# First layer norm scaled on ScalarE with a bias from GpSimd, and low parts of x subtracted on GpSimd

## The reference, cut to what matters

```python
x = _layernorm(x + _L0_attn_ref(x, w_in, w_out), axis=-1)
x = _layernorm(x + _L0_ffn_ref(x, wf, uf, bf, wi, ui, bi, wc, uc, bc, wo, uo, bo, in_c), axis=-1)

def _layernorm(x, axis=-1, eps=1e-05):
    m = jnp.mean(x, axis=axis, keepdims=True)
    v = jnp.var(x, axis=axis, keepdims=True)
    return (x - m) / jnp.sqrt(v + eps)
```

## Time and profile before

| what | value |
|---|---|
| median of 3 runs | 1065.08 us (1063.71 to 1067.06) |
| the profiled execution | 1063.56 us, span 1061.8 us, mean granted clock 0.966 |
| PE busy | 941.6 us, 89% of the span |
| DVE busy | 766.2 us, 72% |
| ACT busy | 551.6 us, 52% |
| POOL busy | 361.9 us, 34% |

### The profile page before, as it was taken

The page is one execution under the profiler, slowest core; times in us unless marked ns, Lnnn a source line. Parts: engine busy times, 40 slices in busy tenths (PEclk is TensorE's granted clock), DMA queues, the critical chain, the costliest instruction groups (busy, mean ns, idle before and its releaser), DMA issues.

```text
span 1061.8 us, 22111 instructions
## 1 busy us (share of the span) xinstructions
PE 941.6 (89%) x7576; PEld 710.8 (67%) x7576; DVE 766.2 (72%) x2882; ACT 551.6 (52%) x1101; POOL 361.9 (34%) x621
## 2 busy tenths in 40 slices
PE   3278899999999999999999999999999989788995
PEld 2155667676767676767676767676767757567884
DVE  6367667878786868686868686868787777336885
ACT  5044545555555555555555555555555454414876
POOL 2024333333333333333333333334343333300443
PEclk9688989999999999999999999999999999899998
DMA  6845353535353544445353536262626240103664
GB/s 191 188 136 153 114 152 92 159 94 157 104 150 111 140 121 119 142 111 151 99 158 93 157 88 160 84 176 81 180 61 165 77 100 2 41 20 99 189 209 139
DMA packets 92942, 131.74 MB, mean 124 GB/s; under 512 B 12008, under 2 KB 46696, under 8 KB 92832
## 3 DMA queue, kind: packets, MB, share of 16 engines
q1 hardware_dynamic: 92832, 130.34, 43.5%
HBM read 78.84 MB, written 50.33 MB: 122 GB/s over the span
## 4 chain that ended last, share of the span: by engine, by line
PE 57%; DVE 17%; ACT 9%; POOL 6%; issue 5%; SPq 3%; DMA 2%; ACTq 0%; POOLq 0%; DVEq 0%
PE bank L868 34%; PE bank L925 8%; PE bank L884 7%; DVE bank L652 5%; PE bank L906 3%; PE bank L933 3%; POOL Pt L348 2%; ACT Pt L427 2%; POOL Pt L350 2%; DVE y L694 2%; PE bank L964 2%; DVE gate L707 2%; DVE max_q L652 1%; ACT oT L444 1%; DVE c L709 1%
## 5 line engine op out<-in xcount | busy, mean ns | idle before, releaser
L652 DVE CUSTOM_DVE_ANT_0 bank<-bank,mask 128x256 f32<-128x256 f32 (+1 forms) x1024 | 368.7, 422 | 155.3 <-PE bank L884 154.1
L348 POOL TENSOR_SCALAR_AFFINE_SELECT Pt<-Pt 128x512 f32<-128x512 f32 x256 | 169.4, 662 | 588.0 <-ACT Pt L427 588.0
L427 ACT ACTIVATE Pt<-bank 128x512 f32<-128x512 f32 (+1 forms) x512 | 250.9, 545 | 170.0 <-PE bank L906 169.9
L884 PE MATMUL bank<-Ks,Qs 58*128 58x256 f32 (+1 forms) x1024 | 141.5, 336 | 43.6 <-DMA Ks<-parts_dram 23.4
L884 PEld LDWEIGHTS bank<-Ks,Qs 58*128 58x128 f32 x1024 | 84.1, 189 | 130.4 <-issue 88.0
L868 PE MATMUL bank<-x1T,Wg 128*128 128x512 f32 x576 | 158.6, 412 | 1.6 <-DVE x1T L625 1.6
L868 PE MATMUL bank<-cT,Ug 128*128 128x512 f32 x576 | 152.0, 401 | 3.7 <-DVE cT L625 3.7
L350 POOL TENSOR_SCALAR_AFFINE_SELECT Pt<-Pt 128x384 f32<-128x384 f32 x256 | 149.3, 583 | 0.0
L652 DVE DVE_READ_ACCUMULATOR2_ANT max_q<- 128x1 f32 x1024 | 144.3, 141 | 0.0
L925 PE MATMUL bank<-Pt,Vp 128*32 128x256 f32 (+1 forms) x2048 | 115.7, 369 | 12.1 <-POOL Pt L350 12.0
L868 PEld LDWEIGHTS bank<-cT,Ug 128*128 128x128 f32 x576 | 106.0, 190 | 26.2 <-DVE cT L625 4.1
(11 more groups left out here) (101 smaller groups left out, 1121.4 us busy)
## 6 DMA issues: line engine op xcount, KB each, us to landing
parts_dram<-qk_parts SPq DMA_DIRECT2D x128, 256.0 KB
Qs<-parts_dram SPq DMA_DIRECT2D x128, 128.0 KB, 2.6
Ks<-parts_dram SPq DMA_DIRECT2D x128, 128.0 KB, 2.8
xt_raw<-in_xt SPq DMA_DIRECT2D x16, 512.0 KB, 3.8
Qs<-parts_dram SPq DMA_DIRECT2D x128, 64.0 KB, 2.6
Ks<-parts_dram SPq DMA_DIRECT2D x128, 64.0 KB, 2.7
x_res<-in_x SPq DMA_DIRECT2D x16, 512.0 KB, 6.1
x_dram<-y SPq DMA_DIRECT2D x16, 512.0 KB, 3.3
```

The lines of the kernel that those rows point to most:

```text
L348: gp.affine_select(out=p4[:, :, 0:128], in_=p4[:, :, 0:128], compare_op=ALU.is_ge, fill=0.0, base=0, pattern=[[0, 4], [1, 128]], channel_m ...
L427: sc.activation(probabilities(g, 2 * pair + odd)[:, S * a:S * a + n], SC[odd][:, 0:n], ACT.Exp).then_inc(exp_done, 1)
L652: ins = ve.tensor_tensor_reduce(out=raw, in0=raw, in1=mask[:, keys], scale=1.0, scalar=MASKED, op0=ALU.add, op1=ALU.max, accum_out=max_q[: ...
L884: ins = te.matmul(MX[odd][:, 256 * (n % 2):256 * (n % 2) + 256][:, keys], Qs[rows, 2 * g + pair, n * WIN:(n + 1) * WIN], Ks[rows, 2 * g + ...
```

## The change

The four scalings of `y` go from DVE to ACT, as `Identity(y * rstd + shift)` with one scale and one bias for each token. POOL makes the bias: after `var_eps` it writes `minus_mean`, then `rstd`, waits for both, and multiplies them into `shift`. On ACT the four instructions stand at the end of an iteration, behind `c_hi(t - 2, 0)`, and in `last_sequences()` between the last `c_hi` of sequence t-1 and `x1_hi(t, 0, X)`. The low parts of x go from DVE to POOL, both blocks between `window(t, 1, 3)` and `inverse_std(t - 1)`, and for sequences 0 and 1 ahead of POOL's loop.

```diff
-        masked_done, vareps_done, rstd_done = sem("masked_done"), sem("vareps_done"), sem("rstd_done")
+        masked_done, vareps_done, rstd_done, shift_done = sem("masked_done"), sem("vareps_done"), sem("rstd_done"), sem("shift_done")
...
                 wait(pool, x1_done, 4, t - 1, 4)
+                gp.tensor_scalar(minus_mean[:, :], mean_var[:, 0, :, 0], -1.0, None, ALU.mult).then_inc(rstd_done, 1)
                 gp.tensor_tensor(rstd[:, 0, :], var_eps[:, :], minus_half[:, :], ALU.pow).then_inc(rstd_done, 1)
+                wait(pool, rstd_done, 2, t, 2)
+                gp.tensor_tensor(shift[:, 0, :], minus_mean[:, :], rstd[:, 0, :], ALU.mult).then_inc(shift_done, 1)
+
+            def x_lo(t, c):
+                wait(pool, xhi_done, 2, t, c + 1)
+                gp.tensor_tensor(xT[:, t % 2, 1, c, :], xt_raw[:, c, :], xT[:, t % 2, 0, c, :].bitcast(F32), ALU.subtract).then_inc(xlo_done, 1)
...
+                if real(t + 2):
+                    x_lo(t + 2, 0)
+                    x_lo(t + 2, 1)
                 if p1: inverse_std(t - 1)
...
+            for t in range(2):
+                for c in range(KC):
+                    x_lo(t, c)
             for t in range(B + 1):
                 iteration(t)
...
+            def layernorm(t):
+                wait(act, shift_done, 1, t, 1)
+                for n in range(NB):
+                    sc.activation(y[:, n, :], y[:, n, :], ACT.Identity, bias=shift[:, 0, n:n + 1],
+                                  scale=rstd[:, 0, n:n + 1]).then_inc(x1_done, 1)
...
                     gates(t - 2, 5, Y)
                     c_hi(t - 2, 0)
+                if p1: layernorm(t - 1)
...
                 c_hi(t - 1, 1)
+                layernorm(t)
                 x1_hi(t, 0, X)
...
-            def x_lo(t, c):
-                wait(dve, xhi_done, 2, t, c + 1)
-                minus_hi(xT[:, t % 2, 1, c, :], xt_raw[:, c, :], xT[:, t % 2, 0, c, :]).then_inc(xlo_done, 1)
-
...
-            def layernorm(t):
-                wait(dve, rstd_done, 1, t, 1)
-                for n in range(NB):
-                    ve.tensor_scalar(y[:, n, :], y[:, n, :], mean_var[:, 0, n, 0:1], rstd[:, 0, n:n + 1],
-                                     ALU.subtract, ALU.mult).then_inc(x1_done, 1)
```

More of the change, by code:

```diff
@@ L749, in iteration @@
                 if now: normalise(t, 0, X)
-                if n2: x_lo(t + 2, 0)
                 attend(12)
@@ L760, in iteration @@
                 attend(14)
-                if n2: x_lo(t + 2, 1)
                 attend(15)
                 if now: normalise(t, 1, Z)
-                if p1: layernorm(t - 1)
             def last_sequences():
@@ L785, in last_sequences @@
                 c_lo(t - 1, 1)
-                layernorm(t)
                 x1_lo(t, 0, X)
@@ L795, in _ @@
             ve.memset(Ks[:, :, :].bitcast(F32), 1.0).then_inc(mem_ready, 1)
-            for c in range(KC):
-                x_lo(0, c)
             weights_lo(0)
@@ L804, in _ @@
             qk_lo(0, 3, X)
-            for c in range(KC):
-                x_lo(1, c)
             dve.wait_ge(small_in, 48)
```

## The result

The changed kernel takes 1105.07 us (median of 4 runs, 1103.15 to 1108.35) against 1065.99 for the kernel before on the same chip: 1.0373 times as long, with a 95% interval of 1.034 to 1.0405. The forecast was 1107, range 1086 to 1116. The profiled execution of the changed kernel has a span of 1101.4 us, 39.6 more than before. In its profile the four scalings are L462, the transposes L967, the products L871, the subtractions on GpSimd L365.

What follows compares the result with a forecast made beforehand. TensorE, 89% busy and in order, was taken as the bound, its slack before y's transposes used up. Later start and ends 23.9 us plus clock falls 18 made 41.9 us: 1107.0 us on the median, range 1086 to 1116.

Steps and rivals of the forecast that it cites:

- Low parts of x: Two subtractions per sequence moved from VectorE to GpSimd: hidden on both, costed at nothing; 1.1 us each, at most 1.9.
- The four small steps: GpSimd's variance, negated mean, power and new product behind the subtractions: 2.8 us with gaps, bias ready at 574.6.
- limit of about 2.2 us: On GpSimd, one subtraction must stay under this length for the bias to be ready before ScalarE can use it.
- Layer norm on ScalarE: At 14 regular iteration ends, scalings start 1.21 us later and take 0.45 longer: 1.65 us each, 23.1 us.
- The clock: TensorE's longer wait for y drops its clock at 12 of 14 regular ends, 1.5 us each: 18 us.
- the prediction's 14 falls by that rule: The Trainium skill's loop, one wait per pass lowering TensorE's clock every pass: falls at all 14 ends, 21 us.
- The rival with a steady clock: Same later start of y at the ends, but no clock falls: 1089.0 us (1086 to 1093), chance 0.28.
- First sequence and start: About 0.4 us for GpSimd's late chain at sequence 0, and 0.4 for VectorE's weight split slowed at the start.
- VectorE without the layer norm: VectorE is 1.63 us earlier at slot 0, but its next work for TensorE needs the transposes: gain nothing.
- the faster one: If ScalarE had y ready before TensorE asks, the 14.2 us of waits would vanish: 1051 us, chance 0.04.
- the prediction's upper bound: GpSimd's subtraction slowed as a masking was beside VectorE on two SBUF operands, factor 1.7: 1.9 us.

Runs made afterwards that it cites:

- the spare products: Changed kernel plus nine spare 512-column products on TensorE just ahead of the transposes of y, adding no result; 1086.38 us, ratio 1.0187 to the kernel before.
- the split: Kernel before with two of four layer-norm scalings on ScalarE ahead of the last gate, with GpSimd's bias, two left on VectorE; 1055.16 us, ratio 0.9923.

## Why the prediction was right, step by step

**Low parts of x.** Costed at nothing on both engines; measured alone, 0.9992. One subtraction takes 1.26 us, inside the bounds of 1.1 and 1.9 and near the value taken. The four small steps take 1.84, not 2.8, with the product at 0.20, not 0.99. So the limit of about 2.2 us for one subtraction was set too low: with each done twice, 2.6 us from one block to the next, the regular ends stood as they were, with 0.04 us to spare.

**Layer norm on ScalarE.** The scalings start 1.11 us after the gate and take 2.06, as read from the earlier trace rows; transposes wait 2.53 us, 1.63 more than before. Forecast 23.1 us for 14 ends; 13 periods have 21.4 of it and the first end 1.65, and with the clock held by the spare products the loss was 21 us in all. That the place makes it, more than the length, is shown by the run with the same instructions ahead of the gate: 42 us from one place to the other, the falls included.

**The clock.** Forecast 12 falls at 1.5 us, 18 us; in the profile 11 falls at 1.46, 16.1 us. The spare products show that the wait is the cause: they change what TensorE does in it and nothing about y, and take 19 us off. The trace has a fall after a wait of 2.53 at 11 of 14 ends, and with the layer norm alone at all 14, one of them after 2.77. So the prediction's 14 falls by that rule carried it over to shorter waits, and its 12 lies between the 11 and the 14 of the two executions. The rival with a steady clock, 1089, is nearly what the spare products made (1086).

**First sequence and start.** 0.8 forecast, and 0.86 between the two traces, but that they agree is luck. The scalings ahead of the gate change nothing up to the first sequence's end, which has no gate, and yet the transposes there stand 3.0 us apart in the two executions (PE, the changed kernel first, then the scalings ahead of the gate):

```profile
138.21 1.94 PE L967 MATMUL bank<-ident,y 128*128 128x128 f32 x8 [0.94 <-ACT y L462]
...
141.21 1.06 PE L967 MATMUL bank<-ident,y 128*128 128x128 f32 x8 [0.95 <-ACT y L462]
```

Nor do the reasons given account for it. At that end GpSimd's bias does come last, as forecast (ScalarE waits 0.23 us for it), but the transposes wait less than before, 0.94 us against 1.32. VectorE's split of the weights was to be 0.4 us slower beside GpSimd's subtractions; in the changed kernel the two never ran together (6.97 to 9.46 the one, from 9.94 the other), and the split took 1.76 us, as before. It began 0.37 us later, since ScalarE's rounding ahead of it waited that much longer for the transfer of the weights (to 8.43 us, 8.06 before). In the run with the low parts alone, where the two overlapped by 0.24 us, the split took 1.85.

**VectorE without the layer norm.** Gain nothing, as forecast. Of the rivals, the faster one had its condition right: the split has y ready before TensorE asks, or nearly, and is faster. That needs the scalings ahead of the gate, which the change as made doesn't do.

The sum of 41.9 us stands against 39.6 in the spans and 39.1 in the medians; the 2.3 too many are the twelfth fall and its price (1.9) and 0.4 that the changed kernel gained behind the last of the transposes.

## What to carry to other kernels

In a list of fixed order, look at what a moved instruction stands behind before its price: four scalings that cost 0.45 us more on the other engine cost 1.65 for each sequence behind a gate, and were free or better ahead of it, in time that the engine spent waiting. When the engine that bounds the kernel is made to wait longer, read its clock after such waits elsewhere in the trace: here the falls of the clock cost 16 us and the longer wait itself 23. Work on an engine that waits for TensorE anyway can be split between two engines so that each part fits into a wait.

## What the runs showed that was not expected

The same wait of 2.53 us with the same work around it put the clock down at 11 ends and not at 2 others of the same execution, 196.72 and 599.95. The place of the fall moved steadily: 0.4 us after the start of the transposes at 253.06, a little later at each end, 1.4 us at 542.20; at 599.95 none came; at 656.30 it stood at their start again, and moved on from there (the transposes at 656.30 and 714.19 above take 1.94 and 1.89 us). What sets that place no row shows.

In the run with doubled subtractions one of them took 2.78 us instead of 1.27, while VectorE split the weights from two SBUF operands; two pairs of rows of that start (timeline, GpSimd and VectorE):

```profile
8.33 1.27 POOL L368 TENSOR_TENSOR xT<-xt_raw,xT 128x512 fp32r<-128x512 f32 x1
9.55 2.78 POOL L366 TENSOR_TENSOR xT<-xt_raw,xT 128x512 fp32r<-128x512 f32 x1
...
9.26 1.96 DVE L649 SCALAR_TENSOR_TENSOR Win<-Pt,Win 128x1536 fp32r<-128x1536 f32 x1 [3.00 <-ACT Win L415]
11.13 1.74 DVE L649 SCALAR_TENSOR_TENSOR Pt<-Pt 16x512 fp32r<-16x512 f32 x1
```

VectorE's large split was slowed by little (1.96 against 1.76), its small one from 0.67 to 1.74. So in this one place company cost GpSimd a factor of 2.2, more than the 1.7 of the prediction's upper bound, VectorE's long instruction 1.1 and its short one 2.6.
